# Key parts in DRAM: stored once and read three times by the load, in a transformer kernel on one core

## What is computed

```python
x = x + xattn(layernorm(x), ctx)      # q = x@Wq, k, v = ctx@Wkv; softmax(q k / sqrt(8)) v; proj
x = x + ffn(layernorm(x))             # with, inside ffn:
#   q, k = rmsnorm(rope(h@Wq)), rmsnorm(rope(h@Wk));  causal softmax(q k / sqrt(8)) v, gated, @Wo
#   top1 = argmax(rmsnorm(x)@Wr);  y = (u1 * sigmoid(u2)) @ W2[top1] + b2[top1]
```

## Time and profile before

| | us |
|---|---|
| runs before | 252.91, 254.10, 254.95 |
| median | 254.1 |
| the profiled execution | 252.22 |
| its span (first to last instruction) | 250.5 |

### The profile page before, as it was taken

How to read it: one execution, slowest core, us unless ns; L and a number is a source line. 1 busy time by engine, 2 the same in 40 slices (tenths; PEclk the granted TensorE clock), 3 DMA queues, 4 the chain that set the end, 5 groups by cost and what they waited for, 6 DMA issues and landing times.

```text
span 250.5 us, 4635 instructions
## 1 busy us (share of the span) xinstructions
PE 183.0 (73%) x1419; PEld 111.7 (45%) x1430; DVE 158.1 (63%) x405; ACT 116.6 (47%) x218; POOL 121.4 (48%) x231
## 2 busy tenths in 40 slices
PE   0668778895897787887876898796885530699991
PEld 0437214553454453543533454453332220698880
DVE  6478695786588786676798777778214252255651
ACT  0535324664354756652553575455361142267650
POOL 4443557026115336746777885526128523035554
PEclk9999999999799999998899799999596555599997
DMA  5364676865744634535025035134351201443000
GB/s 151 106 167 141 180 205 173 214 169 136 227 151 139 201 91 136 178 94 133 3 83 156 4 81 157 38 139 171 124 215 39 87 3 42 124 126 103 26 29 0
DMA packets 22036, 29.69 MB, mean 119 GB/s; under 512 B 3806, under 2 KB 17162, under 8 KB 21142
## 3 DMA queue, kind: packets, MB, share of 16 engines
q1 hardware_dynamic: 20076, 27.31, 37.2%
q0 software_dynamic: 960, 1.59, 1.9%
q10 hardware_dynamic: 976, 0.50, 0.8%
HBM read 14.73 MB, written 14.98 MB: 119 GB/s over the span
## 4 chain that ended last, share of the span: by engine, by line
PE 42%; DVE 18%; DMA 13%; issue 10%; POOL 8%; ACT 5%; SPq 1%; POOLq 1%; another core or an unknown queue 0%; DVEq 0%; ACTq 0%
PE S L1238 13%; PE O L1238 10%; PE MXX L1238 8%; DMA QA<-MTS 7%; PE MS L1238 5%; DVE NEGM L969 5%; DMA X<-in_x 2%; PE MS L1493 2%; DMA k_rows<-PT 1%; DVE ST L957 1%; DVE QKVS L1133 1%; DMA rooms<-HR,PLACE 1%; POOL RQ L677 1%; PE MS L1501 1%; POOL RT L675 1%
## 5 line engine op out<-in xcount | busy, mean ns | idle before, releaser
L969 DVE TENSOR_REDUCE NEGM<-MXX 128x2 f32<-128x512 f32 (+1 forms) x112 | 74.8, 687 | 24.0 <-PE MXX L1238 20.5
L876 ACT ACTIVATE EX<-S 128x1024 f32<-128x1024 f32 x64 | 58.4, 915 | 46.5 <-PE S L1238 45.8
L1238 PE MATMUL MXX<-KA,QA 96*128 96x256 bf16 (+1 forms) x256 | 48.3, 287 | 5.1 <-DVE NEGM L969 2.7
L1238 PE MATMUL S<-QA,KA 128*128 128x256 bf16 (+1 forms) x172 | 36.7, 317 | 8.4 <-DMA QA<-MTS 8.1
L1238 PEld LDWEIGHTS MXX<-KA,QA 96*128 96x128 bf16 x256 | 21.4, 104 | 25.4 <-DVE NEGM L969 12.3
L667 POOL TENSOR_SCALAR_AFFINE_SELECT EX<-EX 128x512 f32<-128x512 f32 x32 | 20.1, 642 | 14.1 <-ACT EX L876 14.1
L1238 PEld LDWEIGHTS S<-QA,KA 128*128 128x128 bf16 x176 | 17.1, 102 | 16.8 <-DMA QA<-MTS 9.7
L1238 PE MATMUL O<-EX,VA 128*32 128x256 f32 x256 | 20.9, 398 | 2.3 <-issue 2.0
L1238 PE MATMUL O<-EX,VB 128*32 128x256 f32 (+1 forms) x256 | 19.1, 373 | 4.4 <-POOL EX L667 2.5
L1048 DVE SCALAR_TENSOR_TENSOR AJ<-S,VA,SJ 128x128 f32<-128x128 f32 x30 | 9.1, 346 | 13.4 <-ACT SJ L820 13.4
L1238 PE MATMUL S<-HJ,VA 128*128 128x128 f32 x120 | 17.6, 295 | 0.0
(11 more groups left out here) (188 smaller groups left out, 324.2 us busy)
## 6 DMA issues: line engine op xcount, KB each, us to landing
rooms<-FILL SPq DMA_DIRECT2D x8, 1028.0 KB, 5.4
QA<-q_rows SPq DMA_DIRECT2D x24, 192.0 KB
k_rows<-PT SPq DMA_DIRECT2D x12, 192.0 KB, 3.4
KA<-k_rows SPq DMA_DIRECT2D x12, 192.0 KB
W<-in_w SPq DMA_DIRECT2D x8, 258.0 KB, 4.6
q_rows<-PT SPq DMA_DIRECT2D x24, 64.0 KB, 2.9
KA<-rooms SPq DMA_DIRECT2D x8, 128.5 KB, 2.1
W<-in_w SPq DMA_DIRECT2D x8, 128.0 KB, 4.3
```

The source lines that it names most:

```text
L876: act.activation(EX[g % PRING][:, 0:w], S[g % 2][:, 0:w], ACT.Exp).then_inc(probs, 1)
L969: dve.tensor_reduce(out=NEGM[:, q, heads[0]:heads[-1] + 1], in_=MX[g % 2][:, 0:len(heads) * w].rearrange("p (h t) -> p h t", t=w), axis=AX ...
L1238: return nc.tensor.matmul(out_, lhsT, rhs, start=start, stop=stop, **kw)
```

## The change

`k_store` writes each key part once, without the dimension of copies. `k_load` reads it three times: its source has a leading dimension of 3 with step 0, then the 8 channels, then the row. The tensors k_rows and k2_rows lose the dimension of copies. The destination, the waits, the semaphores and the order of all issues are as they were.

```diff
             def k_store(e, c):
                 nk, k_e = heads_of_k(e), k_rows[e] if e < B else k2_rows[e - B]
-                sp.dma_start(k_e[c].rearrange("i p t -> p i t"),
-                             PT[e % 2][0:nk * HD, c, 1, None, :].broadcast_to([nk * HD, NPART, T])).then_inc(k_out[c], 16)
+                sp.dma_start(k_e[c], PT[e % 2][0:nk * HD, c, 1, :]).then_inc(k_out[c], 16)
...
                 sp.wait_ge(k_out[c], 16 * (e + 1))
                 sp.dma_start(KA[e % RING][c:ROWS:NPART, 0:nk, :].rearrange("p h t -> p (h t)"),
-                             k_e[c].rearrange("i (d h) t -> (i d) (h t)", h=nk)).then_inc(k_stacked[e % RING], 16)
+                             k_e[c].rearrange("(d h) t -> d (h t)", h=nk)[None, :, :]
+                             .broadcast_to([NPART, HD, nk * T])).then_inc(k_stacked[e % RING], 16)
...
-    k_rows = nc.dram_tensor("k_rows", [B, NPART, NPART, H * HD, T], bf16, kind="Internal").ap()
-    k2_rows = nc.dram_tensor("k2_rows", [B, NPART, NPART, G * HD, T], bf16, kind="Internal").ap()
+    k_rows = nc.dram_tensor("k_rows", [B, NPART, H * HD, T], bf16, kind="Internal").ap()
+    k2_rows = nc.dram_tensor("k2_rows", [B, NPART, G * HD, T], bf16, kind="Internal").ap()
```

## The result

The changed kernel takes 271.23 us (median of four runs, 269.78 to 274.2) against 254.07 us (four runs too), 17.2 us more. The forecast was 262.5 us with 255 to 269 us as its range. The direction was right, and so was the step on which it hung, the three engines; the forecast's 8.5 us were half of what came, and the time lies above the range.

What follows compares the result with a forecast made beforehand. It took the kernel as bound not by bandwidth but by waits for small maxima transfers that land with the stack loads. Terms 5 + 2 + 1.5 + 1 - 1 = +8.5 us on 254.1 us gave about 262.5 us, range 255 to 269.

Steps and rivals of the forecast that it cites:

- the three engines: Key loads: with 3 as the source's first dimension, each load runs on three DMA engines instead of twelve.
- the price of a load: Key loads: 0.31 to 0.42 us per 8 KB packet, engines busy 1.9 to 2.5 us longer; one stack 10.2 to 13.9 us.
- The rule that the maxima transfer lands with the loads around it: Maxima transfers into QA: whatever makes a stack load last longer makes the maxima late.
- Items 1 and 2: e = 0 and 1: last query load 2 us late, then key store and first scores late; +5 us together, 2 to 7.
- Item 3: Second maxima transfer, between the loads of e = 2, whose issue waits for late stores: +2 us, 0 to 4.
- Item 4: Maxima transfer at 56.17 us: its burst grows to up to 13.9 us, but ScalarE is later too; +1.5 us, 0 to 4.
- The clock: TensorE's granted clock: longer waits may bring more low-clock stretches; no size given, left in the high end.
- Item 5: From e = 4 on, rows of 2 KB: 0.5 us more a load, two long maxima transfers; +1 us, 0.5 to 2.
- Item 6: Query and key stores write one copy instead of three and are shorter: -1 us, -2 to 0.
- twelve engines: Rival: key loads stay on twelve engines or go to eight, only shorter stores count; about 252.5 us, chance 0.10.
- hidden: Rival: key loads use three engines, but stacks still land before they are needed; about 254.5 us, chance 0.08.
- the worst case: Rival: packets of the first four maxima transfers alternate with 8 KB ones, 10 us beside the +8.5; about 272 us, chance 0.07.

Runs made afterwards that it cites:

- experiment 5: Kernel before with e = 3 loads issued after the fourth maxima transfer: 0.992; also the first fill moved to the end: 0.996; changed kernel with late loads: 1.066.
- once_e3: The kernel before with the change applied for e = 3 only: 1.018 (1.011 to 1.026) times the kernel before.
- experiment 7: Changed kernel with 16 extra matmuls ahead of the first score matmul in three places where TensorE waits for the maxima: 1.070 times the kernel before.
- once_e4_on: The kernel before with the change applied for e = 4 to 7 only: 1.017 (1.007 to 1.027) times the kernel before.

## Why the prediction was half right

- **The three engines** and the price of a load: right. Three engines, 0.32 us for a packet in the burst and 0.42 us in the mixed loads of e = 1, against 0.31 to 0.42 us. The burst for e = 3 runs from its first issue at 67.14 to the landing beside 81.75 us; from 1.7 us behind the issue that is 12.9 us, within the 10.2 to 13.9 us.
- **The rule that the maxima transfer lands with the loads around it**: right as far as the neighbours make it long (experiment 5). How they do was wrong, and that is the step that failed: the sum gave the transfer no cost of its own beside its neighbours, and took packets that alternate for a rival with a chance of 0.07. They do alternate. Of the 10.30 us of the fourth transfer, 4.8 us pass before its first packet (4.6 us of 6.60 before) and 5.1 us from its first packet to its last, one behind each 8 KB packet, where it was 1.5 us. In the second it is 2.8 us (0.4 us before), in the first 1.8 us (0.6 us before), and in once_e3, whose transfer takes 10.97 us, 5.4 us. What holds back the first packet no run here takes apart.
- **Items 1 and 2, the first scores, +5 us with 7 us as the high end**: +8.0 us. The wait of TensorE for the last query load ends at 28.74 us, 2.8 us later (forecast 2). The loads of e = 1 went nearly as priced at the slower rate: their packets of 8 KB begin at 31.1 us (forecast 30.4) and end at 44.8 us, 33 on each slow engine, 0.42 us each (forecast end 40.6 to 44.3). SP issues the last two of these loads 5.1 us later, yet the slow engines do not stand empty: three packets or more are under way at every moment from 31.3 to 44.5 us, near 36 us those of the store (512 bytes) that SP waits for. What failed is the comparison behind that: item 2 set the end of the loads against 38.70 us, when the scores began before, as if both fell together. Before, the loads' last packet ended at 36.9 us, 1.8 us ahead of the scores; now it is 1.9 us. With that the +2 to +5.6 us would have been +3.7 to +7.4.
- **Item 3, the second transfer, +2 us**: 8.34 against 3.79 us, +4.6 us, beyond the high end of 4. The term was mis-sized: the transfer lies behind the loads of two parts, 22 packets on a slow engine instead of 10, so its first packet begins 4.7 us after the issue instead of 2.5, and it alternates behind that.
- **Item 4, +1.5 us**: 10.30 against 6.60 us, +3.7 us, and 4.4 us in once_e3. The thought was that ScalarE would be later by as much as the burst's start and so not wait longer. Both hang on the same scores and move together (the first load of the burst was issued at 52.52 us and the transfer at 56.17 us, 3.7 us apart; now at 67.14 and 71.45 us, 4.3 us apart), so nearly the whole lengthening of the burst, 8.6 to 12.9 us by the same count, falls on the transfer. The prediction had the burst before at 6.3 us at most.
- **The clock**, left in the high end without a number: 12.4 us from 59.03 to 71.45 us, where it was 9.7 us from 46.47 to 56.17 us, +2.7 us. That this is the wait's doing is suggested and not shown (experiment 7).
- These four give 8.0 + 4.6 + 2.7 + 3.7 = 19.0 us by 82 us, the whole of the span's 19.1 us, where the forecast had 5 + 2 + 0 + 1.5. The shifts stood in the right places; each was priced at about half or less, and all to the same side. I had written that all high ends at once are unlikely. They are not independent: all four hang on the same three engines' backlog.
- **Item 5, e = 4 on**: +1 us forecast; from 19.0 us at 82 us the distance grows to 20.3 us at the last maxima transfer, +1.3, and that is back to 19.1 us by the end; once_e4_on has none of it in its trace and 1.7% in its time, which stays open. **Item 6**: right.
- **The rivals**: twelve engines and hidden are refuted by the packet counts and the scores' start. The mechanism of the worst case, packets that alternate, is there in the second and fourth transfers, 2.8 and 5.1 us, at about the price it was given (16 packets of 0.31 us, 5 us). It was counted for all four and on top of the 8.5 us, so that its 272 us lie beside the measured 271.23 us is in part luck: the true sum is the one above.

## What to carry over

A DMA's cost is set by how many engines its pattern lets it use as much as by its bytes: here 1.9 MB fewer written cost 17 us, because a dimension of 3 came to the front of a load's source. Before a broadcast or a copy is folded into a pattern, look at the first dimension of both sides; the number of packets that begin together shows in the trace what it got. A small transfer that shares an engine with large ones has a price of its own: here each of its 16 packets on an engine let one of 8 KB pass, 0.33 us a turn. And don't treat the high ends of terms with one common cause as independent.

## What I had not expected

- A small transfer on another queue (8 KB from ScalarE's) waits behind the SP queue's traffic: 2.0 us with none beside it, 3.5 to 6.6 us before, 6.7 to 10.3 us beside loads on three engines. In the longest, half of the time is its packets taking turns with those of 8 KB.
- TensorE's granted clock can be low for a long stretch at no visible cost. Over the stretch from 20 to 40 us the kernel before ran at 1.00 and once_e3, which does the same there, at 0.50, yet the first scores began at 38.70 and 37.68 us; that stretch waits for transfers. These are the two slices:

```profile
20.00:40.00 20.00, 15.23 (x58) 7.93 (x59) 14.25 (x21) 6.44 (x20) 11.78 (x19) 1.00 0.63 167
```

```profile
20.00:40.00 20.00, 15.32 (x61) 7.78 (x60) 14.65 (x23) 6.71 (x18) 12.09 (x24) 0.50 0.64 174
```
